# Graph attention in a four-layer GNN kernel: in three of eight units of three heads ScalarE writes the rectified difference and TensorE adds the logarithms of the counts

## The reference

```
def _gat_conv(x, src, dst, W, a_s, a_d, b):
    h = (x @ W).reshape(n, H, C)
    al_s = (h * a_s).sum(-1)
    al_d = (h * a_d).sum(-1)
    e = jax.nn.leaky_relu(al_s[src] + al_d[dst], 0.2)
    m = jax.ops.segment_max(e, dst, num_segments=n)
    ex = jnp.exp(e - m[dst])
    denom = jax.ops.segment_sum(ex, dst, num_segments=n)
    msg = h[src] * (ex / denom[dst])[:, :, None]
    return jax.ops.segment_sum(msg, dst, num_segments=n).reshape(n, H * C) + b

h = relu(layernorm(gat_conv(x)))    # round 0
h = relu(layernorm(gat_conv(h)))    # round 1
h = gat_conv(h)                     # round 2
```

## Time and profile before

| | us |
|---|---|
| median of 3 runs | 1013.98 |
| profiled execution, its own time | 1013.37 |
| its span | 1011.5 |
| busy: TensorE / VectorE / ScalarE / GpSimd | 834.6 / 695.8 / 476.0 / 316.5 |
| `sloped`, L975, 96 of 1290 ns | 121.7 |
| `greatest`, L964, 96 of 1219 ns | 113.4 |
| exp, L630, 96 of 1113 ns | 106.5 |

### The profile page before, as it was taken

One profiled execution on the slowest core, in us unless ns is written; L12 is line 12 of the kernel. 1 busy time (PEld: TensorE's weight loads), 2 busy tenths in 40 slices (PEclk: granted clock), 3 DMA queues, 4 the chain that ended last, 5 costly groups with the idle time before them and its releaser, 6 DMA issues.

```text
span 1011.5 us, 18259 instructions
## 1 busy us (share of the span) xinstructions
PE 834.6 (83%) x5207; PEld 523.3 (52%) x5236; DVE 695.8 (69%) x1803; ACT 476.0 (47%) x979; POOL 316.5 (31%) x424
## 2 busy tenths in 40 slices
PE   3999969989898989898989796877877766776658
PEld 2556738868787878686868644411142112311124
DVE  6399986666666666666666763699568875998451
ACT  5232105555555555564546655354544544445421
POOL 5030047545444545454535400122233120122000
PEclk9999969999999999999999999799879997999879
DMA  3120032111111111111112200000000000000300
GB/s 79 39 68 1 1 124 64 47 57 52 52 51 53 52 57 47 62 42 62 47 57 46 58 1 1 1 0 1 0 1 1 1 0 1 0 1 0 129 38 21
DMA packets 19139, 35.76 MB, mean 35 GB/s; under 512 B 5281, under 2 KB 11553, under 8 KB 18977
## 3 DMA queue, kind: packets, MB, share of 16 engines
q0 software_dynamic: 7104, 19.41, 6.7%
q1 hardware_dynamic: 12000, 15.95, 4.7%
HBM read 29.56 MB, written 5.79 MB: 35 GB/s over the span
## 4 chain that ended last, share of the span: by engine, by line
PE 63%; DVE 21%; ACT 6%; issue 5%; POOL 4%; DMA 0%; DVEq 0%; POOLq 0%; ACTq 0%
DVE OHd L964 9%; PE PS L1225 7%; PE PS L1147 6%; PE PS L1148 6%; PE PS L1219 5%; PE PS L1162 5%; DVE PS L975 5%; PE PS L1097 4%; PE PS L1337 4%; PE PS L1140 3%; PE PS L1262 3%; PE PS L1216 3%; PE PS L1153 2%; PE PS L1298 2%; PE PS L1328 2%
## 5 line engine op out<-in xcount | busy, mean ns | idle before, releaser
L390 POOL DMA_INDIRECT BT<-Qtab,gidx x148 | 150.5, 1017 | 96.3 <-DVE gidx L789 61.2
L537 ACT ACTIVATE OHe<-OHs,sew 128x128 bf16<-128x128 bf16 x408 | 126.7, 389 | 56.1 <-PE PS L1225 52.6
L404 POOL TENSOR_SCALAR KV<-BT,pid 128x256 bf16<-128x256 uint8 x74 | 70.3, 950 | 180.0 <-DVE MS L864 175.2
L964 DVE CUSTOM_DVE_ANT_0 OHd<-PS,n1T 128x1024 bf16<-128x1024 f32 x96 | 113.4, 1219 | 18.6 <-PE PS L1298 18.6
L549 ACT ACTIVATE m2s<-m2s 128x512 f32<-128x512 f32 x68 | 42.8, 630 | 119.1 <-DVE m2s L891 119.1
L1328 PE MATMUL PS<-rowA,sel 128*128 128x512 bf16 x177 | 57.9, 407 | 48.6 <-DVE PS L975 38.6
L443 POOL TENSOR_TENSOR zl<-AL,Sx 128x8 f32<-128x8 f32 x12 | 11.3, 946 | 258.7 <-DVE Sx L964 258.7
L891 DVE TENSOR_TENSOR m2s<-PS,bm 128x512 f32<-128x512 f32 x68 | 47.0, 691 | 59.0 <-PE PS L1148 58.8
L905 DVE TENSOR_SCALAR OHd<-iotaN,dstf 128x1024 bf16<-128x1024 f16 x136 | 64.6, 515 | 33.2 <-PE PS L1225 33.2
L1147 PE MATMUL PS<-Wm,m1T 128*128 128x256 f32 x272 | 83.8, 391 | 0.0
L1148 PE MATMUL PS<-Wm,m1T 128*128 128x256 f32 x272 | 82.6, 386 | 0.0
(11 more groups left out here) (342 smaller groups left out, 1668.7 us busy)
## 6 DMA issues: line engine op xcount, KB each, us to landing
BT<-Wtab SPq DMA_DIRECT2D x1, 4096.0 KB, 12.9
BT<-Qtab,gidx POOLq DMA_INDIRECT x148, 2.8
BT<-Stab SPq DMA_DIRECT2D x1, 2048.0 KB, 10.2
Wtab<-H SPq DMA_DIRECT2D x4, 512.0 KB, 2.8
Wtab<-cs SPq DMA_DIRECT2D x4, 512.0 KB, 2.9
Qtab<-BT SPq DMA_DIRECT2D x1, 1024.0 KB, 4.5
Wn<-in_L_gnn_Wn SPq DMA_DIRECT2D x1, 1024.0 KB, 5.5
x<-in_x SPq DMA_DIRECT2D x1, 512.0 KB, 4.3
```

Of the source, the lines that this page charges most:

```text
L390: g.indirect_dma_start(out=G[:, p % SLOTS, k, :], out_offset=None, in_=Qtab, in_offset=bass.IndirectOffsetOnAxis(ap=gidx[:, p, k:k + 1], a ...
L537: a.activation(OHe[:, k, j, :], OHs[:, k, :], ACT.Copy, scale=sew[:, j, bass.ds(2 * g + k, 1)])
L964: v.tensor_tensor_reduce(junk[n % 2], bank(4, 2), mask[:, i, :], 1.0, 2 * FAR, ALU.subtract, ALU.max, Sx[:, i, hd:hd + 1]).then_inc(S("gat ...
```

## The change

In the units 1, 3 and 5 of heads 0, 1 and 2 (9 of a round's 32, 27 in all) VectorE no longer writes the tile. Since max(drow, 0.8 s) = relu(drow - 0.8 s) + 0.8 s, ScalarE writes relu(`drow` + `n8`) to PSUM, with the new column `n8` = -0.8 s as bias; TensorE adds `LNC` by two fp32 matmuls against the identity, 512 columns each; and the exp of such a unit takes s (`AL`) as bias where it had 0.2 s. On ScalarE `ramp(hd, j + 1)` stands ahead of the exp of unit j. The `greatest` of the next head get new places in all heads: two each after units 0, 1 and 2, one each after units 3 and 4. VectorE has one small instruction more a round, for `n8`. SyncE waits on `gat_rowed` for the last reading of `LNC`.

```diff
+RAMPED = (1, 3, 5)
+        n8 = sb("n8", [P, NB, HEADS])
+        ramped = lambda n: n // NB % HEADS < HEADS - 1 and n % NB in RAMPED
+        ramps = [sum(ramped(i) for i in range(n + 1)) for n in range(3 * HEADS * NB)]
+        maxes = [n + 1 - ramps[n] for n in range(3 * HEADS * NB)]
...
-            eng.wait_ge(S("gat_tt"), HEADS * NB * 3)
+            eng.wait_ge(S("gat_rowed"), HEADS * NB * 3)
             eng.dma_start(BT[:], Wtab.rearrange("(b p) n -> p b n", p=P)).then_inc(S("BT_loaded"), 16)
...
+                def ramp(hd, j):
+
+                    n = HEADS * NB * l + NB * hd + j
+                    if not ramped(n):
+                        return
+                    if n >= 2:
+                        eng.wait_ge(S("gat_ec"), n - 1)
+                    a.activation(tile(hd, j), drow[hd], ACT.Relu, bias=n8[:, j, hd:hd + 1]).then_inc(S("gat_ramp"), 1)
+
+                eng.wait_ge(S("cols_ready"), l + 1)
+                eng.wait_ge(S("banks_clear"), l + 1)
...
+                        if j + 1 < NB:
+                            ramp(hd, j + 1)
                         eng.wait_ge(S("gat_rowed"), n + 1)
...
-                        a.activation(EC[n % 4], tile(hd, j), ACT.Exp, bias=s2[:, j, hd:hd + 1])\
+                        shift = AL if ramped(n) else s2
+                        a.activation(EC[n % 4], tile(hd, j), ACT.Exp, bias=shift[:, j, hd:hd + 1])\
...
+                v.tensor_scalar(n8[:], AL[:, :, 0:HEADS], SLOPE - 1.0, None, ALU.mult)
...
-                first = {1: (0, 1, 2, 3), 2: (4,), 3: (5,), 4: (6,), 5: (7,)}
-                later = {1: (0, 1), 2: (2, 3), 3: (4, 5), 4: (6,), 5: (7,)}
+                between = {0: (0, 1), 1: (2, 3), 2: (4, 5), 3: (6,), 4: (7,)}
                 for hd in range(HEADS):
                     for j in range(NB):
-                        sloped(hd, j)
+                        if not ramped(HEADS * NB * l + NB * hd + j):
+                            sloped(hd, j)
...
                 def bounded(hd, j):
...
-                    eng.wait_ge(S("gat_tt"), n + 1)
+                    if ramped(n):
+                        eng.wait_ge(S("gat_ramp"), ramps[n])
+                        for half in range(2):
+                            t.matmul(tile(hd, j)[:, half * BANK:(half + 1) * BANK], ident[:],
+                                     LNC[:, j, half * BANK:(half + 1) * BANK],
+                                     start=False, stop=False, skip_group_check=True)
+                    else:
+                        eng.wait_ge(S("gat_tt"), maxes[n])
```

More of the change, by code:

```diff
@@ L991, in _ @@
                 link(v.tensor_scalar(s8[:], AL[:, :, 0:HEADS], 1.0 - SLOPE, None, ALU.mult))
+                v.tensor_scalar(n8[:], AL[:, :, 0:HEADS], SLOPE - 1.0, None, ALU.mult)
                 v.tensor_scalar(s2[:], AL[:, :, 0:HEADS], SLOPE, None, ALU.mult).then_inc(S("cols_ready"), 1)
                 eng.wait_ge(S("cols_ready"), l + 1)
-                first = {1: (0, 1, 2, 3), 2: (4,), 3: (5,), 4: (6,), 5: (7,)}
-                later = {1: (0, 1), 2: (2, 3), 3: (4, 5), 4: (6,), 5: (7,)}
+                between = {0: (0, 1), 1: (2, 3), 2: (4, 5), 3: (6,), 4: (7,)}
                 for hd in range(HEADS):
                     for j in range(NB):
-                        sloped(hd, j)
+                        if not ramped(HEADS * NB * l + NB * hd + j):
+                            sloped(hd, j)
                         if hd + 1 < HEADS:
-                            for i in (later if hd else first).get(j, ()):
+                            for i in between.get(j, ()):
                                 greatest(hd + 1, i)
```

## The result

| | before | after |
|---|---|---|
| median, us | 1013.59 (1013.17 to 1014.08) | 1002.51 (1001.41 to 1002.98) |
| profiled execution, us | 1013.37 | 1001.41 |
| its span, us | 1011.5 | 999.6 |
| mean granted clock | 0.947 | 0.958 |

The ratio of the times is 0.9889, with an interval from 0.9872 to 0.9906: 1.1% faster. The forecast was 1002.8.

A forecast was written before the change was run, and what follows sets the result against it. VectorE was taken to bound most of the attention, TensorE nearly throughout after the change. Heads -11.2, round starts -1.5 and half clock +1.5 sum to -11.2 us from 1013.37: 1002.2, named 1002.8 by the median; range 999 to 1009.

The forecast's parts named there:

- L on TensorE, 1.82 us: Ramped units: the two new fp32 identity matmuls hold TensorE 1.82 us at full clock, 16.4 us a round.
- The cheaper row, `summed` with 0.98: Ramped units: rival that the identity matmuls run like summed, 0.98 us; some 3 us less a round, 993.5; chance 0.05.
- The Relu, 1.1 us: Ramped units: ScalarE's Relu of 1024 columns to PSUM with a bias column takes 1.1 us.
- Heads 0 to 3, 20.4, 21.4, 19.7 and 15.9: Attention: head lengths in us with TensorE as bound at full clock; 77.4 us a round, together -11.2 us.
- The wait of 0.56 us for the first Relu: Head 0: TensorE waits 0.56 us, since ScalarE does the first Relu only behind the copy to rowA.
- The clock ahead of head 3: Head 3: full clock instead of half gives some 4.8 us, 1.8 in round 0 and about 1.5 in each other.
- The rival that it would not come back, 1007.6: Head 3: TensorE's clock stays low from idles or short waits, 4.8 us of gain stay away; chance 0.22.
- The chain ahead of head 3: Handover to head 3: maxima end beside unit 4, some 8 us early, so GpSimd's chain of 7.45 us or less fits.
- The round's start, -0.5 each: Round's start: GpSimd's chain loses about 1.0 us, TensorE then waits for ScalarE's last drow copy; 0.5 taken, -1.5 in all.
- Half a clock for the first L, +1.5 in round 0: Round 0's start: the first new identity matmuls meet half clock, most of a doubling, +1.5 us.
- New waits: Ramped units: rival that queue waits of 0.4 us for each of 27 units eat 11 us, 1013.6, no change; chance 0.07.
- The price of a slow Relu: Heads 0 to 2: rival that ScalarE's PSUM write is dear; gain gone near 1.75 us, 1020 at 2.0; chance 0.08.

The follow-up runs named there:

- doubled: The changed kernel with the two fp32 matmuls of LNC run twice in each ramped unit; ratio 1.0327 to the kernel before, rounds of 92.51 us.
- the filled wait in the kernel before: The kernel before, with fourteen unused bf16 matmuls of zeros filling TensorE's wait ahead of head 3; ratio 0.9962.
- what the wait gave in the kernel before: The kernel before, with VectorE's first sloped of head 3 waiting until GpSimd's chain for head 3 is done; ratio 0.9890.
- with two: The changed kernel with only units 1 and 3 of a head ramped, not 1, 3 and 5; ratio 0.9885 to the kernel before, 1002.66 us.
- two of the runs: The changed kernel with units 1 and 3 ramped (1002.66 us), and with one, two, two and no ramped units without the added wait (1000.18 us).
- one, two and two units in heads 0 to 2: The changed kernel with unit 3 of head 0, units 1 and 3 of heads 1 and 2 ramped, VectorE waiting for GpSimd's chain ahead of head 3; 0.9746.
- an L of two pieces: The changed kernel with LNC's upper 16 bits added by two bf16 matmuls against a bf16 identity; ratio 0.9717 to the kernel before.

## Why the prediction was right, step by step

- **L on TensorE, 1.82 us.** Right: 1.82 from start to start, and 1.72 when doubled, from the same shape in the earlier trace rows. The cheaper row, `summed` with 0.98, was rightly set aside.
- **The Relu, 1.1 us.** Right: 27 of them at 1112 to 1119 ns. ScalarE's write to PSUM costs what the exp costs from PSUM to SBUF, 1.11. The estimate of 1.13 us by the Trainium skill (ScalarE: Activation LUTs, What ACT_TABLE_LOAD costs) agrees.
- **Heads 0 to 3, 20.4, 21.4, 19.7 and 15.9.** Measured 20.20 (without the half clock below), 21.33, 19.61 to 19.78, and 15.92 to 15.93. The wait of 0.56 us for the first Relu was 0.40 us.
- **The clock ahead of head 3.** Right: 1.00 in 712 to 716 and in 717 to 723. The rival that it would not come back, 1007.6, had its condition refuted. Head 3 is shorter by 1.79, 1.26 and 1.29 us, 4.3 in all, for the 4.8 named; the filled wait in the kernel before gives the same 15.92. The prediction had not seen the falls to 0.50 inside heads 1 and 2 of the kernel before, listed with the filled wait above; after has none there. They had cost little: head 1 took 21.68 us with one and 21.49 without.

  The Trainium skill (TensorE: Matmul & The Clock Gate, A second HAM failure mode: psum-queue depth-cycling) warned of short idles between groups. The prediction set it aside by one stretch, 771 to 774. These falls mean that it isn't refuted here: the kernel with idles in its units has one in each round, and after, nearly without them, has 1.00 in all of rounds 0 and 1. No run shows that the short idles are the cause.
- **The chain ahead of head 3.** The result fits, the reason doesn't. The text said that the maxima end beside unit 4 and that 7.45 us or less then fit. The run with the new places alone had a chain of 8.6 us and gained nothing; the one with old places and ramps gained everything. The lead was also shorter than the 8 us named, 6.96 us (706.19 to 713.15): a chain of 7.45 us would have kept TensorE waiting for 0.5 us, and that it took 3.6 us was not foreseen. What counts is how much VectorE runs `sloped` beside the chain: after has one stretched instruction, since VectorE waits for the exps there, and the run with places alone has six. It was the weakest step, and some 4 us a round hung on it (what the wait gave in the kernel before), so that it held with three units was in part luck: with two it fails, and the forecasts for two of the runs were wrong by it.
- **The round's start, -0.5 each.** Right in size and in the reason: GpSimd's chain has one stretched instruction for two before, and TensorE is released by ScalarE's last copy (`cs`, part of `drow`), in round 1 after 0.69 us, where it had waited 1.31 us for GpSimd:

```profile
757.55 0.62 PE L1338 MATMUL PS<-identb,Apad 128*128 128x128 bf16 x8 [0.69 <-ACT cs L602]
```

- **Half a clock for the first L, +1.5 in round 0.** The place was wrong, the size was right. Round 0 had 1.00 in 657 to 660. In round 2 it came, at 0.50 in 866 to 868: one L of 3.2 us from start to start, and head 0 at 21.90 for 20.20.

```profile
865.00 3.42 PE L1349 MATMUL PS<-BT,ident 128*128 128x512 f32 x4 [0.40 <-ACT PS L632]
868.21 0.90 PE L1355 MATMUL PS<-rowA,sel 128*128 128x512 bf16 x2
```

  What decides whether a round has it stays open: in the run with the old places it was round 1, and in each of these it is the first L of head 0.
- **New waits.** VectorE waits 51 us for the exps, and it costs nothing, since TensorE is last meanwhile: the doubled L came through in full.
- **The price of a slow Relu.** The text's own numbers don't agree: by a loop that hides exactly at 1.1 us and loses 0.9 us a round for each 0.1 us, the gain would be used up at 1.5 us a Relu, not 1.75, and 2.0 us would cost 8.1 us a round, not 5.8. At the 1.12 us measured it had no part.
- **`n8`, the load of `BT`.** Nothing, as said: 11.7 of 11.9 us are in the rounds and at their starts.

## What to carry to other kernels

Giving work to another engine pays until that one is last: nine L cost TensorE 16.4 us a round to take 10.8 from VectorE, and with the chain out of the way one, two and two units in heads 0 to 2 do better than three each (0.9746 for 0.9887). Look at who runs beside the small chain that hands over to the next stage; here three instructions that nobody needed yet, together with the half clock that followed the wait for them, cost as much as the whole change won, and one wait took that loss away. Two edits that each remove the same wait don't add, so run each part alone before crediting the whole.

## What the runs showed of the hardware

A GpSimd instruction of 128 x 8 takes 0.20 to 0.26 us alone and 1.06 to 1.31 us beside VectorE's `sloped`, two fp32 operands from SBUF over 1024 columns, unless it starts within 0.03 us of it (0.20 to 0.27 us). Beside `greatest`, which reads PSUM and a bf16 tile and writes an SBUF tile, it keeps its 0.2 us, as at the start of round 1 of after:

```profile
755.59 0.22 POOL L456 CAST Apad<-Acol 128x8 bf16<-128x8 f32 x1
755.88 0.20 POOL L459 TENSOR_TENSOR Acol<-Acol,Apad 128x8 f32<-128x8 f32 x1
...
755.19 1.23 DVE L983 CUSTOM_DVE_ANT_0 OHd<-PS,n1T 128x1024 bf16<-128x1024 f32 x1 [0.33 <-PE PS L1318]
```

The Trainium skill (GPSIMD Engine Reference, Specifications) says that GpSimd shares its SBUF interfaces with VectorE and that they contend when VectorE has two SBUF inputs. The trace agrees; the size, a wait for about the rest of the VectorE instruction, is from these rows. A bf16 operand read with a step of two elements cost no more than a dense one: 0.47 us for an L of two pieces against 0.52 us for `bounded`'s two.
